# Layer 2 attention: the order of the transfers, of GpSimd's keys and values, and the tiles in which VectorE and ScalarE norm the values

## The chip, the cores and the metric

The kernel runs on one core of a Trainium2 chip, in one launch. The metric is the device time in microseconds (us), taken as the median of the executions shown. The engines are TensorE (PE; its weight loads are shown apart, as PEld), VectorE (DVE), ScalarE (ACT), GpSimd (POOL) and SyncE (SP), which issues the transfers that the 16 DMA engines carry out.

## The reference, cut to what matters

The model is four layers of cross attention and feed-forward on `x` (16 batches, 56 rows, 128 columns), with a context `ctx_1024` of 1500 rows for each batch. The change touches only the attention of layer 2:

```python
xn = _ln(x, ln1_s, ln1_b)
cn = _ln(context, lnc_s, lnc_b)      # every context row: minus its mean, over its deviation
q = xn @ Wq
k, v = jnp.split(cn @ Wkv, 2, axis=-1)
...                                   # 16 heads of 64; one null key and null value in front
sim = jnp.einsum('bhid,bhjd->bhij', q * scale, k)
attn = softmax(where(mask, sim, max_neg))
out = jnp.einsum('bhij,bhjd->bhid', attn, v)
return _ln(out @ Wo, lno_s, lno_b)
```

The kernel folds the weights into the queries and into the output, so that it attends straight to the normed context: the keys are the normed context turned (128 by 1500), the values the normed context as it lies (1500 by 128).

## The kernel before, in words

The 16 heads of 56 queries of a batch are 896 rows, or seven tiles of 128, so the 16 batches make 112 tiles. The 1500 context rows of a batch are 12 chunks of 125 rows. A chunk is cut into four windows: window 0, 1 and 2 have 32 rows, window 3 has the 29 that are left (`LAST_KEYS`) and the null row. A buffer `V` holds the values of one batch: four quadrants of 32 partitions with the same rows in each, and 48 blocks, 12 for each window.

Each of TensorE, VectorE and ScalarE runs one loop over 120 passes. In pass n TensorE makes the scores of tile n (8 matmuls, `scores`, L1628), then one seventh of the weighted sum of the batch that lies eight tiles back (`weigh`, L1647, 56 or 48 small matmuls, the blocks in their order). VectorE takes the maximum of tile n (L1837), turns tile n-1 (L1854), inverts the sum of tile n (L1859), and then norms a window of values if one is due. ScalarE takes the exponentials of tile n (L1764), scales it (L1769), and norms its part of the same window. The scores of a tile wait for the maximum of the tile before it (one PSUM bank). A window of values is normed by three engines: GpSimd takes five chunks of its 12, VectorE three, ScalarE four, in place in `V`. In which pass VectorE and ScalarE do so is set by `values_due`; GpSimd runs a list of its own.

SP issues every transfer in one written order and waits in that order. The waits are these:

- `load_values(b, w)` (L1559) waits until the blocks of window w of the batch before have been weighed, since `V` is one buffer; it is four DMAs, one for each quadrant, of 32 rows, and of 29 rows for window 3.
- `load_keys(b)` (L1573) waits until the scores of batch b-2 are done (two buffers); it is a DMA of 112 rows and one of 15.
- `load_moments(b)` (L1581) brings the means and the reciprocal deviations, spread over all partitions, into single buffers, and waits until GpSimd has normed the keys of batch b-1.
- `load_mask(b)` (L1565) waits until ScalarE has made the mask of batch b-1.

GpSimd norms the keys of a batch with two instructions over 1500 columns (L1713, L1715), and its five chunks of a window with one copy and five instructions (L1720, L1723).

**Words used below.** The cycle of batch v runs from the issue of its window 3 to the issue of window 3 of batch v+1. SP issues it when TensorE has ended the last seventh of batch v-1. Counted from there, TensorE weighs batch v in passes 1 to 7 of the cycle: pass 1 needs window 0, pass 2 window 1, pass 4 window 2 and pass 6 window 3. A pass of TensorE starts a seventh only when all three engines have normed each window that it touches.

The line that says in which pass a window is normed before (n counts all passes, RT is 7):

```python
b, t = divmod(n - RT - 5, RT)
return [(b + 1, t // 2)] if 0 <= b and b + 1 < B and t % 2 == 0 else []
```

In passes of a cycle this is: window 2 of batch v in pass 2, window 3 in pass 4, window 0 of batch v+1 in pass 5, window 1 in pass 7.

Of the kernel before, what the change touches and what calls it, by code (L numbers as in the profile page):

```python
# [14 lines left out]
B, Q, S2 = 16, 56, 1500  # L15
# [101 lines left out]
def ln_pool(pool, k, s):  # L117
    nc = k.nc
    for h in range(2):
        pool.wait_ge(s.ln_var, h + 1)  # L120
        nc.gpsimd.tensor_tensor(k.rstd[:, 4 * h:4 * h + 4], k.mv[:, 4 * h:4 * h + 4, 1], k.half_neg[0:TT, 0:4],
                                ALU.pow).then_inc(s.ln_rstd, 1)
# [768 lines left out]
class LatentAhead:  # L891
# [24 lines left out]
    def load_mask(self, sp, b):  # L916
        sp.dma_start(self.MR[:, b % 2, :], self.src["mask_some"][b].partition_broadcast(TT)).then_inc(self.mask_loaded[b % 2], 16)
# [477 lines left out]
RT = 7  # L1395
WINDOWS = 4
# [76 lines left out]
def attention_16_wide_heads(nc, k, src, ahead):  # L1473
# [8 lines left out]
    with ExitStack() as ctx:  # L1482
# [55 lines left out]
        def values_due(n):  # L1538
            if n < WINDOWS:
                return [(0, n)]  # L1540
            b, t = divmod(n - RT - 5, RT)
            return [(b + 1, t // 2)] if 0 <= b and b + 1 < B and t % 2 == 0 else []

        def step_blocks(g):
            return range(RT * g, min(RT * g + RT, BLOCKS))
# [3 lines left out]
        @block.sync  # L1549
        def _(sp):  # L1550
            def load_values(b, w):
                if b:
                    last_step = (NCH * w + NCH - 1) // RT
                    sp.wait_ge(s.pv_done, RT * (b - 1) + last_step + 1)
                else:
                    sp.wait_ge(s.v_zeroed, 1)
                n = BW if w < WINDOWS - 1 else LAST_KEYS
                for a in range(4):
                    sp.dma_start(V[a * BW:a * BW + n, w * NCH:(w + 1) * NCH, :], src["ctx"][b][w * BW:w * BW + n]  # L1559
                                 ).then_inc(values_loaded[w], 16)  # L1560

            def load_mask(b):
                if b:
                    sp.wait_ge(s.mask_ready, 2 * b)
                sp.dma_start(MR[:], src["mask_full"][b].partition_broadcast(P)).then_inc(s.mask_loaded, 16)  # L1565

            def load_keys(b):
                if b < 2:
                    sp.wait_ge(s.slot_ready, 2 * b + 2)
                else:  # L1570
                    sp.wait_ge(s.scores_filled, RT * (b - 1))
                for rows in (slice(0, TT), slice(TT, P - 1)):
                    sp.dma_start(KT[rows, b % 2, 0:S2], src["ctxT"][b][rows]).then_inc(keys_loaded[b % 2], 16)  # L1573

            def load_moments(b):
                if b == 1:
                    sp.wait_ge(s.q_filled, 2 * H)
                if b:
                    sp.wait_ge(s.keys_scaled, b)
                for x, to in enumerate((MEAN[:], scale_of(b))):  # L1580
                    sp.dma_start(to, scratch[x, b].rearrange("c n -> (c n)").partition_broadcast(P)).then_inc(s.spread_loaded, 16)  # L1581

            load_mask(0)
            load_keys(0)
            sp.wait_ge(s.moments_ready, 1)
            sp.dma_start(scratch.rearrange("k (h b) c n -> (b c) (k h) n", h=2), MOMENTS).then_inc(s.moments_stored, 16)
            sp.wait_ge(ahead.s.means_ready, 1)
            sp.wait_ge(ahead.s.spread, B)
            sp.wait_ge(s.stats_zeroed, 1)
            sp.wait_ge(s.moments_stored, 16)  # L1590
            load_moments(0)
            for x, of in enumerate((ahead.means, rs)):
                for w in range(WINDOWS):
                    n = BW if w < WINDOWS - 1 else LAST_KEYS
                    for a in range(4):
                        sp.dma_start(VST[a * BW:a * BW + n, x, w], of[w * BW:w * BW + n]).then_inc(s.stats_spread, 16)
            load_values(0, 0)
            for a in range(4):
                at = a * BW + LAST_KEYS
                sp.dma_start(V[at:at + 1, BLOCKS - 1, :], k.ident[P - 1:P, :]).then_inc(s.null_rows, 16)  # L1600
            load_values(0, 1)
            load_keys(1)
            load_values(0, 2)
            load_values(0, 3)
            load_moments(1)
            load_mask(1)
            load_mask(2)
            for b in range(1, B):
                if b + 1 < B:
                    load_keys(b + 1)  # L1610
                    load_moments(b + 1)
                for w in range(WINDOWS):
                    if w == WINDOWS - 1 and b + 2 <= B - 1:
                        load_mask(b + 2)
                    load_values(b, w)

        @block.tensor
        def _(pe):
# [86 lines left out]
        @block.gpsimd  # L1705
        def _(pool):
            def normalise_keys(b):
                pool.wait_ge(keys_loaded[b % 2], 32 * (b // 2 + 1))
                pool.wait_ge(s.spread_loaded, 32 * (b + 1))
                if b == 0:  # L1710
                    pool.wait_ge(s.slot_ready, 4)
                keys = KT[0:P - 1, b % 2, 0:S2]
                nc.gpsimd.tensor_tensor(keys, keys, MEAN[0:P - 1], ALU.subtract).then_inc(s.keys_moved, 1)  # L1713
                pool.wait_ge(s.keys_moved, b + 1)
                nc.gpsimd.tensor_tensor(keys, keys, scale_of(b)[0:P - 1], ALU.mult).then_inc(s.keys_scaled, 1)  # L1715

            def normalise_values(b, w):
                pool.wait_ge(values_loaded[w], 64 * (b + 1))
                blocks = slice(w * NCH, (w + 1) * NCH)
                nc.gpsimd.tensor_copy(V[:, blocks, P - 1:P], NULL[:, blocks].unsqueeze(2))  # L1720
                for c in POOL_CHUNKS:
                    x = V[:, w * NCH + c, 0:P - 1]
                    last = nc.gpsimd.tensor_scalar(x, x, VST[:, 1, w, b, c:c + 1], VST[:, 0, w, b, c:c + 1], ALU.mult, ALU.add)  # L1723
                last.then_inc(s.v_pool, 1)

            for u in range(2):
                nc.gpsimd.memset(KT[:, u, :], 0.0).then_inc(s.slot_ready, 1)
                pool.wait_ge(s.slot_ready, 2 * u + 1)
                nc.gpsimd.tensor_copy(KT[:, u, S2:S2 + 1], k.ident[:, P - 1:P]).then_inc(s.slot_ready, 1)
                if u == 0:  # L1730
                    ln_pool(pool, k, s)
                    pool.wait_ge(s.ln_rstd, 2)
            nc.gpsimd.memset(VST[:, :, WINDOWS - 1], 0.0).then_inc(s.stats_zeroed, 1)
            nc.gpsimd.memset(V[:, (WINDOWS - 1) * NCH:, :], 0.0).then_inc(s.v_zeroed, 1)
            nc.gpsimd.memset(BIG[:], FLT_MAX).then_inc(s.constants, 1)
            for u in range(2):
                nc.gpsimd.memset(MA[:, u, WINDOWS - 1, :, LAST_KEYS:BW], FLT_MAX).then_inc(s.margins, 1)
            for u in range(2):
                pool.wait_ge(s.margins, u + 1)
                nc.gpsimd.memset(MA[:, u, WINDOWS - 1, NCH - 1, LAST_KEYS:LAST_KEYS + 1], 0.0).then_inc(s.margins, 1)  # L1740
            pool.wait_ge(s.margins, 4)
            normalise_keys(0)
            pool.wait_ge(s.offsets_ready, 1)
            pool.wait_ge(s.null_column, 2)
            pool.wait_ge(s.null_rows, 64)
            normalise_values(0, 0)
            normalise_values(0, 1)
            normalise_keys(1)
            normalise_values(0, 2)
            normalise_values(0, 3)  # L1750
            for b in range(1, B):
                if b + 1 < B:
                    normalise_keys(b + 1)
                for w in range(WINDOWS):
                    normalise_values(b, w)
            ln_pool(pool, k, s2)

        @block.scalar
        def _(act):
# [51 lines left out]
            for n in range(TILES + LAG):  # L1811
                b, t = divmod(n, RT)
                if n < TILES:
                    exp(n)
                if n >= LAG and (n - LAG) % RT == RT - 1:
                    take_heads((n - LAG) // RT)
                if n < TILES:
                    scale(n)
                if t == (2 if b == 0 else 5) and b + 1 < B:
                    mask(b + 1)  # L1820
                if n == 0:
                    act.wait_ge(s.offsets_ready, 1)
                for v in values_due(n):
                    normalise_values(*v)
# [901 lines left out]
```

## Time and profile before

| | us |
|---|---|
| median of 3 runs | 2388.59 (2386.11 to 2388.67) |
| time of the profiled execution | 2392.87 |
| its span | 2391.1 |
| PE busy / DVE / ACT / POOL | 2023.3 / 1519.9 / 1354.4 / 902.6 |

The span runs from the first to the last instruction; the time has 1.8 us around it. The mean granted TensorE clock is 0.902 of full speed. Layer 2's loop over the tiles lies between 893.7 and about 1816 us of the span.

How rows are read: in the views in order of time a row has its start, its length, engine, line, operation, what it writes and reads, and the count of instructions joined in the row; the brackets hold the idle time of the engine just before it and what ended that. In the view by line, the busy time and the mean time (ns) of one instruction come first, then the idle time before all of them with what ended it. In the view of stretches a row has the bounds, the length, the busy time of PE, PEld, DVE, ACT and POOL with counts of instructions, the granted clock (PEclk, a share of full speed), the mean busy share of the 16 DMA engines and their GB/s. In the list of transfers a row has the count, the size of one and the median us to landing.

### The profile page before, as it was taken

To read this page: it belongs to the slowest core of one execution; us is meant where nothing else is said; L and a number is where in the kernel's file an instruction comes from. 1 tells how busy PE (TensorE), PEld (TensorE's weight loads), DVE (VectorE), ACT (ScalarE), POOL (GpSimd) and SP (SyncE) were. 2 spreads that over 40 slices of the span, in tenths; PEclk is the share of its full clock that TensorE was granted. 3 is DMA by queue.
4 is the path that set the end of the run, shared out by engine and by line. 5 is a ranking of instruction groups with operands and counts; after the bars stand their busy time and mean duration, and the time that the engine had idled before them with its cause. 6 is when DMAs were issued, how large, how long until landed. Compare 5 with 4: busy or idle time off the path is not lost. (4 is left out here: it accounts for less than half of the span.)

```text
span 2391.1 us, 52296 instructions
## 1 busy us (share of the span) xinstructions
PE 2023.3 (85%) x21121; PEld 1414.8 (59%) x21121; DVE 1519.9 (64%) x2958; ACT 1354.4 (57%) x2425; POOL 902.6 (38%) x728
## 2 busy tenths in 40 slices
PE   6999999669998995977777777777785979999996
PEld 3777777458874563645455555555563447777774
DVE  5777778689865435655555565555541667777784
ACT  5787787436662226655556555555540247777763
POOL 7656562057764632122223333222210053434410
PEclk7999999679998987988888888888898879999998
DMA  6454543234412142433333333333320144444430
GB/s 167 139 154 138 145 135 95 76 83 138 125 44 73 36 112 82 114 96 95 96 95 97 94 109 96 94 94 94 92 59 6 36 138 136 141 128 135 128 94 9
DMA packets 105519, 240.03 MB, mean 100 GB/s; under 512 B 45688, under 2 KB 54928, under 8 KB 105024
## 3 DMA queue, kind: packets, MB, share of 16 engines
q1 hardware_dynamic: 105280, 236.69, 34.9%
q8 instruction: 168, 2.75, 0.5%
q14 instruction: 71, 0.58, 0.1%
HBM read 155.38 MB, written 0.65 MB: 65 GB/s over the span
## 5 line engine op out<-in xcount | busy, mean ns | idle before, releaser
L1628 PE MATMUL L2ps<-L2keys,L2qz 128*128 128x384 f32 x896 | 382.3, 576 | 206.1 <-DVE L2negmax L1837 206.0
L1628 PEld LDWEIGHTS L2ps<-L2keys,L2qz 128*128 128x128 f32 x896 | 186.0, 218 | 360.7 <-DVE L2negmax L1837 218.6
L1647 PE MATMUL L2ps<-L2work,L2values 32*128 32x224 f32 x6144 | 325.3, 358 | 21.6 <-POOL L2values L1723 15.8
L1647 PEld LDWEIGHTS L2ps<-L2work,L2values 32*128 32x128 f32 x6144 | 287.9, 188 | 87.9 <-issue 54.8
L1764 ACT ACTIVATE L2work<-L2work,L2negmax 128x1536 f32<-128x1536 f32 x112 | 176.0, 1571 | 164.1 <-DVE L2negmax L1837 164.1
L1854 DVE STREAM_TRANSPOSE L2work<-L2work 128x1568 f32<-128x1568 f32 x112 | 202.6, 1809 | 85.0 <-PE L2ps L1647 83.3
L1837 DVE CUSTOM_DVE_ANT_0 L2work<-L2ps,L2maskadd,L2big 128x1536 f32<-128x1536 f32 x112 | 203.3, 1815 | 77.9 <-PE L2ps L1628 74.3
L1846 DVE TENSOR_SCALAR L2values<-L2values,L2value_stats 128x127 f32<-128x127 f32 x192 | 105.8, 607 | 215.7 <-DMA L2values<-in_ctx 215.7
L1720 POOL COPY L2values<-L2null_column 128x12 f32<-128x12 f32 x64 | 13.1, 204 | 602.1 <-DMA L2values<-in_ctx 585.8
L654 ACT ACTIVATE L3probsT<-L3ps 128x448 f32<-128x448 f32 x384 | 196.1, 547 | 70.9 <-PE L3ps L511 66.4
L654 ACT ACTIVATE L0probsT<-L0ps 128x448 f32<-128x448 f32 x384 | 198.2, 552 | 47.8 <-PE L0ps L511 46.7
L1769 ACT ACTIVATE L2work<-L2work,L2rinv 128x1536 f32<-128x1536 f32 x112 | 176.7, 1577 | 84.1 <-DVE L2rinv L1859 83.9
L1775 ACT ACTIVATE L2values<-L2values,L2value_stats 128x127 f32<-128x127 f32 x256 | 104.4, 481 | 155.1 <-DMA L2values<-in_ctx 155.1
L798 DVE TENSOR_REDUCE L0partmax<-L0ps 112x1 f32<-112x1000 f32 x128 | 153.4, 1198 | 58.8 <-PE L0ps L484 56.7
L798 DVE TENSOR_REDUCE L3partmax<-L3ps 112x1 f32<-112x1000 f32 x128 | 153.4, 1198 | 57.8 <-PE L3ps L484 55.5
L1723 POOL TENSOR_SCALAR L2values<-L2values,L2value_stats 128x127 f32<-128x127 f32 x320 | 147.3, 472 | 0.0
L511 PEld LDWEIGHTS L0ps<-L0query_stack,L0key_stack 99*128 99x128 bf16 x1536 | 110.5, 99 | 56.7 <-issue 12.9
L511 PEld LDWEIGHTS L3ps<-L3query_stack,L3key_stack 98*128 98x128 bf16 x1536 | 110.4, 99 | 54.5 <-issue 13.6
L511 PE MATMUL L0ps<-L0query_stack,L0key_stack 99*128 99x112 bf16 x1536 | 133.7, 214 | 1.3 <-ACT L0probsT L654 1.3
L511 PE MATMUL L3ps<-L3query_stack,L3key_stack 98*128 98x112 bf16 x1536 | 133.2, 214 | 0.0
L605 POOL TENSOR_TENSOR L3keys<-L3keys,L3key_parts 128x1500 f32<-128x1500 f32 x16 | 48.6, 3037 | 193.1 <-ACT L3key_parts L701 193.1
L793 DVE TENSOR_REDUCE L0partmax<-L0ps 112x1 f32<-112x500 f32 x128 | 86.2, 674 | 32.7 <-PE L0ps L476 32.7
(484 smaller groups left out, 4075.1 us busy)
## 6 DMA issues: line engine op xcount, KB each, us to landing
L2values<-in_ctx SPq DMA_DIRECT2D x192, 192.0 KB, 3.8
L0key_stack<-L0key_parts SPq DMA_DIRECT2D x192, 187.5 KB
L3key_stack<-L3key_parts SPq DMA_DIRECT2D x192, 187.5 KB
L0ctxT<-in_ctxT SPq DMA_DIRECT2D x16, 750.0 KB, 4.3
L1rawT<-in_ctxT SPq DMA_DIRECT2D x16, 750.0 KB, 6.5
L2mean_spread<-L_moments SPq DMA_DIRECT2D x16, 750.0 KB, 7.4
L3ctxT<-in_ctxT SPq DMA_DIRECT2D x16, 750.0 KB, 4.5
L2wqk<-L_moments SPq DMA_DIRECT2D x15, 750.0 KB, 27.1
```

The costliest lines, as they stand in the source:

```text
L511: last = nc.tensor.matmul(PS[:, bank, c * TT:(c + 1) * TT], KS[:, h % 4, tau, key_columns(4 * j + c)], QS[:, h % 4, tau, :], start=True, s ...
L654: ins = nc.scalar.activation(PT[:, h % 2, 4 * j:4 * j + 4, tau, :], PS[:, bank, 0:HALF].rearrange("p (c n) -> p c n", c=4), ACT.Exp)
L798: nc.vector.tensor_reduce(PM[:, h % 2, tau, 1:2], PS[0:TT, 1:3, 0:500], AX.XY, ALU.max).then_inc(s.m12_done, 1)
L1628: last = nc.tensor.matmul(PS[:, score_bank(m) + w, 0:NCH * BW], tile_rows(m), key_window(b, w), start=True, stop=True)
L1647: last = nc.tensor.matmul(PS[:, 4 + a, 0:RT * BW], V[a * BW:(a + 1) * BW, n, :], block_cells(a, b, n), start=n == 0, stop=n == BLOCKS - 1, ...
L1723: last = nc.gpsimd.tensor_scalar(x, x, VST[:, 1, w, b, c:c + 1], VST[:, 0, w, b, c:c + 1], ALU.mult, ALU.add)
L1764: nc.scalar.activation(SM[:, m % 2, 0:NPR], SM[:, m % 2, 0:NPR], ACT.Exp, bias=nmax[:, m % 4:m % 4 + 1], scale=-1.0, accum_out=ssum[:, m % ...
L1769: nc.scalar.mul(SM[:, m % 2, 0:NPR], SM[:, m % 2, 0:NPR], rinv[:, m % 4:m % 4 + 1]).then_inc(s.scaled, 1)
L1775: last = nc.scalar.activation(x, x, ACT.Identity, bias=VST[:, 0, w, b, c:c + 1], scale=VST[:, 1, w, b, c:c + 1])
L1837: nc.vector.tensor_tensor_reduce(SM[:, m % 2, 0:NPR].rearrange("p (w n) -> p w n", w=WINDOWS), PS[:, bank:bank + 4, 0:NCH * BW], MA[:, m / ...
L1846: last = nc.vector.tensor_scalar(x, x, VST[:, 1, w, b, c:c + 1], VST[:, 0, w, b, c:c + 1], ALU.mult, ALU.add)
L1854: nc.vector.transpose(turned_cells(b, t), SM[:, m % 2].rearrange("p (g r n) -> p g r n", g=RT, n=BW)).then_inc(s.turned, 1)
```

## The change

No instruction is added or removed. SP's list, GpSimd's list and the passes of `values_due` are put in another order.

```diff
--- before.py
+++ after.py
@@ -1538,8 +1538,8 @@
         def values_due(n):
             if n < WINDOWS:
                 return [(0, n)]
-            b, t = divmod(n - RT - 5, RT)
-            return [(b + 1, t // 2)] if 0 <= b and b + 1 < B and t % 2 == 0 else []
+            b, t = divmod(n - RT - 6, RT)
+            return [(b + 1, (0, 2, 4, 5).index(t))] if 0 <= b and b + 1 < B and t in (0, 2, 4, 5) else []
 
         def step_blocks(g):
             return range(RT * g, min(RT * g + RT, BLOCKS))
@@ -1604,15 +1604,23 @@
             load_values(0, 3)
             load_moments(1)
             load_mask(1)
+            load_moments(2)
             load_mask(2)
-            for b in range(1, B):
+            for b in range(1, B + 1):
+                ahead_of = b + 2 < B
                 if b + 1 < B:
                     load_keys(b + 1)
-                    load_moments(b + 1)
-                for w in range(WINDOWS):
-                    if w == WINDOWS - 1 and b + 2 <= B - 1:
-                        load_mask(b + 2)
-                    load_values(b, w)
+                if b >= 2:
+                    load_values(b - 1, 2)
+                    load_values(b - 1, 3)
+                if b < B:
+                    load_values(b, 0)
+                if ahead_of:
+                    load_moments(b + 2)
+                if b < B:
+                    load_values(b, 1)
+                if ahead_of:
+                    load_mask(b + 2)
 
         @block.tensor
         def _(pe):
@@ -1748,11 +1756,15 @@
             normalise_keys(1)
             normalise_values(0, 2)
             normalise_values(0, 3)
-            for b in range(1, B):
+            for b in range(1, B + 1):
                 if b + 1 < B:
                     normalise_keys(b + 1)
-                for w in range(WINDOWS):
-                    normalise_values(b, w)
+                if b >= 2:
+                    normalise_values(b - 1, 2)
+                    normalise_values(b - 1, 3)
+                if b < B:
+                    normalise_values(b, 0)
+                    normalise_values(b, 1)
             ln_pool(pool, k, s2)
 
         @block.scalar
```

SP, from one batch to the next in the middle of the loop. Before, it issues the keys (two DMAs), the moments (two), windows 0 to 2 of the values (twelve), the mask, and window 3 (the four of 29 rows):

```order
L1573 DMA L2keys<-in_ctxT 112x1500
L1573 DMA L2keys<-in_ctxT 15x1500
L1581 DMA L2mean_spread<-L_moments 128x1500
L1581 DMA L2wqk<-L_moments 128x1500
L1559 DMA L2values<-in_ctx 32x1536 x12
L1565 DMA L2mask<-in_mask_full 128x1500
L1559 DMA L2values<-in_ctx 29x1536 x4
```

After, the keys are followed by window 2 and window 3 of one batch, window 0 of the next, the moments for the batch after that, window 1, and the mask:

```order
L1573 DMA L2keys<-in_ctxT 112x1500
L1573 DMA L2keys<-in_ctxT 15x1500
L1559 DMA L2values<-in_ctx 32x1536 x4
L1559 DMA L2values<-in_ctx 29x1536 x4
L1559 DMA L2values<-in_ctx 32x1536 x4
L1581 DMA L2mean_spread<-L_moments 128x1500
L1581 DMA L2wqk<-L_moments 128x1500
L1559 DMA L2values<-in_ctx 32x1536 x4
L1565 DMA L2mask<-in_mask_full 128x1500
```

So window 3 no longer stands ahead of the keys and the moments but between the keys and window 0; the moments are asked for one batch earlier and stand behind window 0.

ScalarE, from the pass in which it takes the weighed heads out of PSUM (the copies; pass 7 of a cycle), before. The rows with 128x127 are norms, those of 128x1536 the exponentials and the scaling of a tile:

```order
L1781 COPY L2qz<-L2ps 128x7x32 x4
L1769 ACTIVATE L2work<-L2work,L2rinv 128x1536
L1775 ACTIVATE L2values<-L2values,L2value_stats 128x127 x4
L1764 ACTIVATE L2work,L2sums<-L2work,L2negmax 128x1536
L1769 ACTIVATE L2work<-L2work,L2rinv 128x1536
L1764 ACTIVATE L2work,L2sums<-L2work,L2negmax 128x1536
L1769 ACTIVATE L2work<-L2work,L2rinv 128x1536
L1775 ACTIVATE L2values<-L2values,L2value_stats 128x127 x4
L1764 ACTIVATE L2work,L2sums<-L2work,L2negmax 128x1536
L1769 ACTIVATE L2work<-L2work,L2rinv 128x1536
L1764 ACTIVATE L2work,L2sums<-L2work,L2negmax 128x1536
L1769 ACTIVATE L2work<-L2work,L2rinv 128x1536
```

And after:

```order
L1793 COPY L2qz<-L2ps 128x7x32 x4
L1781 ACTIVATE L2work<-L2work,L2rinv 128x1536
L1776 ACTIVATE L2work,L2sums<-L2work,L2negmax 128x1536
L1781 ACTIVATE L2work<-L2work,L2rinv 128x1536
L1787 ACTIVATE L2values<-L2values,L2value_stats 128x127 x4
L1776 ACTIVATE L2work,L2sums<-L2work,L2negmax 128x1536
L1781 ACTIVATE L2work<-L2work,L2rinv 128x1536
L1776 ACTIVATE L2work,L2sums<-L2work,L2negmax 128x1536
L1781 ACTIVATE L2work<-L2work,L2rinv 128x1536
L1787 ACTIVATE L2values<-L2values,L2value_stats 128x127 x4
L1776 ACTIVATE L2work,L2sums<-L2work,L2negmax 128x1536
L1781 ACTIVATE L2work<-L2work,L2rinv 128x1536
```

Window 1 is normed in pass 1 in place of pass 7 of the cycle before, window 2 in pass 3 in place of pass 2. Window 3 stays in pass 4 and window 0 moves from pass 5 to pass 6. VectorE's norms stand in the same passes as ScalarE's.

GpSimd, at the start of the loop, from the keys of batch 2 on. Before, four windows follow the keys:

```order
L1713 TENSOR_TENSOR L2keys<-L2keys,L2mean_spread 127x1500
L1715 TENSOR_TENSOR L2keys<-L2keys,L2wqk 127x1500
L1720 COPY L2values<-L2null_column 128x12
L1723 TENSOR_SCALAR L2values<-L2values,L2value_stats 128x127 x5
L1720 COPY L2values<-L2null_column 128x12
L1723 TENSOR_SCALAR L2values<-L2values,L2value_stats 128x127 x5
L1720 COPY L2values<-L2null_column 128x12
L1723 TENSOR_SCALAR L2values<-L2values,L2value_stats 128x127 x5
L1720 COPY L2values<-L2null_column 128x12
L1723 TENSOR_SCALAR L2values<-L2values,L2value_stats 128x127 x5
```

After, two windows follow (0 and 1 of batch 1), and then the next keys:

```order
L1721 TENSOR_TENSOR L2keys<-L2keys,L2mean_spread 127x1500
L1723 TENSOR_TENSOR L2keys<-L2keys,L2wqk 127x1500
L1728 COPY L2values<-L2null_column 128x12
L1731 TENSOR_SCALAR L2values<-L2values,L2value_stats 128x127 x5
L1728 COPY L2values<-L2null_column 128x12
L1731 TENSOR_SCALAR L2values<-L2values,L2value_stats 128x127 x5
L1721 TENSOR_TENSOR L2keys<-L2keys,L2mean_spread 127x1500
L1723 TENSOR_TENSOR L2keys<-L2keys,L2wqk 127x1500
```

From there on GpSimd norms the keys of batch v+2 ahead of window 2 and 3 of batch v; before, it normed them behind window 3.

## Rows read from the trace of the kernel before

**Rows 1.** Groups by line, tile loop, 893.7 to 1816.2 us.

```profile
L1628 PE MATMUL L2ps<-L2keys,L2qz 128*128 128x384 f32 x896 | 382.3, 576 | 206.1 <-DVE L2negmax L1837 206.0
...
L1846 DVE TENSOR_SCALAR L2values<-L2values,L2value_stats 128x127 f32<-128x127 f32 x192 | 105.8, 607 | 215.7 <-DMA L2values<-in_ctx 215.7
```

**Rows 2.** VectorE in order of time, 1293 to 1314 us.

```profile
1295.21 0.12 DVE L1859 RECIPROCAL L2rinv<-L2sums 128x1 f32<-128x1 f32 x1
...
1306.29 0.86 DVE L1846 TENSOR_SCALAR L2values<-L2values,L2value_stats 128x127 f32<-128x127 f32 x3 [10.96 <-DMA L2values<-in_ctx]
...
1313.64 5.36 DVE L1846 TENSOR_SCALAR L2values<-L2values,L2value_stats 128x127 f32<-128x127 f32 x3 [2.86 <-DMA L2values<-in_ctx]
```

**Rows 3.** SP's transfers in order of time, 1262 to 1328 us.

```profile
1270.61 4.14 SPq L1559 DMA_DIRECT2D L2values<-in_ctx  x4
1274.80 8.70 SPq L1573 DMA_DIRECT2D L2keys<-in_ctxT  x2
...
1286.61 32.55 SPq L1559 DMA_DIRECT2D L2values<-in_ctx  x12
...
1327.90 3.91 SPq L1559 DMA_DIRECT2D L2values<-in_ctx  x4
```

**Rows 4.** Stretches: busy by engine, granted clock, DMA share, GB/s.

```profile
1271.40:1281.80 10.40, 10.40 (x127) 7.38 (x125) 7.41 (x11) 8.24 (x15) 0.00 (x0) 1.00 0.07 26
...
1300.00:1305.80 5.80, 0.00 (x0) 0.00 (x0) 0.00 (x0) 0.00 (x0) 0.00 (x0) 0.88 0.06 26
```

**Rows 5.** TensorE in order of time, 1265 to 1345 us.

```profile
1265.16 2.91 PE L1628 MATMUL L2ps<-L2keys,L2qz 128*128 128x384 f32 x8 [2.38 <-DVE L2negmax L1837]
...
1308.94 5.49 PE L1628 MATMUL L2ps<-L2keys,L2qz 128*128 128x384 f32 x8 [9.90 <-DVE L2negmax L1837]
...
1320.79 4.56 PE L1628 MATMUL L2ps<-L2keys,L2qz 128*128 128x384 f32 x8 [3.40 <-DVE L2negmax L1837]
...
1339.19 2.92 PE L1628 MATMUL L2ps<-L2keys,L2qz 128*128 128x384 f32 x8
1342.04 2.93 PE L1647 MATMUL L2ps<-L2work,L2values 32*128 32x224 f32 x56
```

**Rows 6.** SP issues the last window: batches 1, 14 and 15.

```profile
986.46 3.36 SPq L1559 DMA_DIRECT2D L2values<-in_ctx  x4
...
1730.07 4.62 SPq L1559 DMA_DIRECT2D L2values<-in_ctx  x4
...
1777.22 3.85 SPq L1559 DMA_DIRECT2D L2values<-in_ctx  x4
```

**Rows 7.** VectorE norms those windows: batches 14 and 15.

```profile
1763.88 0.85 DVE L1846 TENSOR_SCALAR L2values<-L2values,L2value_stats 128x127 f32<-128x127 f32 x3 [9.10 <-DMA L2values<-in_ctx]
...
1807.08 0.86 DVE L1846 TENSOR_SCALAR L2values<-L2values,L2value_stats 128x127 f32<-128x127 f32 x3 [25.24 <-DMA L2values<-in_ctx]
```

**Rows 8.** Transfers issued, 986 to 1730 us: count, size, landing.

```profile
L2values<-in_ctx SPq DMA_DIRECT2D x156, 192.0 KB, 3.6
...
L2wqk<-L_moments SPq DMA_DIRECT2D x13, 750.0 KB, 27.1
...
L2keys<-in_ctxT SPq DMA_DIRECT2D x13, 656.2 KB, 11.6
```

**Rows 9.** ScalarE in order of time, 1343 us.

```profile
1342.77 1.63 ACT L1775 ACTIVATE L2values<-L2values,L2value_stats 128x127 f32<-128x127 f32 x4
```

**Rows 10.** Stretches, for the granted clock (columns as in 4).

```profile
1304.40:1314.60 10.20, 5.66 (x12) 2.78 (x16) 5.44 (x8) 7.09 (x11) 5.27 (x7) 0.50 0.06 27
...
1260.00:1304.00 44.00, 36.65 (x432) 26.09 (x432) 26.92 (x33) 24.12 (x33) 10.22 (x20) 1.00 0.46 122
```

**Rows 11.** GpSimd in order of time, 1306 to 1318 us.

```profile
1311.86 3.37 POOL L1713 TENSOR_TENSOR L2keys<-L2keys,L2mean_spread 127x1500 f32<-127x1500 f32 x1 [3.01 <-DMA L2wqk<-L_moments]
1315.31 3.36 POOL L1715 TENSOR_TENSOR L2keys<-L2keys,L2wqk 127x1500 f32<-127x1500 f32 x1
```

## The prediction

> **What bounds the kernel now.** First I read the groups by line over layer 2's loop. TensorE stands idle 206.1 us before its scores, nearly all of it until VectorE's maximum; and VectorE stands idle 215.7 us before its norms of values, all of it until a transfer of values lands [rows 1]. So the loop waits for transfers, through VectorE. Next VectorE in order of time, in one cycle: it is free at 1295.33, waits 10.96 us for window 3, norms it at 1306.29, goes through one tile, and waits another 2.86 us for window 0 of the next batch, whose norm then takes 5.36 us where window 3's took 0.86 [rows 2].
>
> SP's own order says when these were asked for: window 3 at 1270.61, so it takes 35.7 us to land; the keys, the moments and window 0 (1286.61) follow, and the next window 3 comes at 1327.90 [rows 3]. Why so long? In the stretches in which nothing else moves the DMA engines are busy for 0.07 and 0.06 of their time, at 26 GB/s; one of 16 is 0.06. In the last of these stretches no compute engine does anything [rows 4]. So window 3 runs on one DMA engine: 4 x 29 rows x 6144 B = 713 KB at 26 GB/s are 27.4 us, and everything asked for later with a share on that engine lands behind it.
>
> This case is one for a rule of the Trainium skill ("DMA: Bandwidth & Descriptors", section "Why a DMA increments its semaphore by 16 and not by 1"): a transfer is spread over the largest number of engines up to 16 that divides its outer size, which for 29 is 1. It speaks against the change, which leaves the 29 rows as they are. With the page's rate of some 27 GiB/s the window alone would take an estimated 24.6 us in place of 27.4, and my sum below would be about 13 x 2.8 = 36 us lower; the measured rate decides.
>
> TensorE's own work is the other bound. In undisturbed passes it goes without a gap: scores from 1339.19, weighing from 1342.04, 2.85 + 2.86 = 5.71 us a pass [rows 5]. Seven are 40.0 us at most, against a cycle of (1730.07 - 986.46)/13 = 57.2 us [rows 6]. So some 17 us of each cycle are to be had at most.
>
> **The change, in one cycle.** I count from the issue of window 3 (time 0) to its landing (L), and from L to the next issue.
>
> *0 to L.* The wait on which SP issues window 3 is the same as before. What changes is what moves beside it. Before: keys, moments, window 0 and 1, with 35.7 us to landing. Batch 14's window 3 has only window 0 and 1 beside it (no further keys or moments exist), and takes 1763.88 - 1730.07 = 33.8 us [rows 6, 7]. Batch 15's, with nothing after it, takes 1807.08 - 1777.22 = 29.9 us [rows 6, 7]. After the change it is window 0, moments, window 1; the keys go ahead of it. By size, keys are 656 + 88 (15 rows of 6000 B) KB and moments 2 x 750 KB, so the moments are two thirds of what they add together [rows 8]: L = 33.8 + 2/3 x 1.9 = 35.1 us, between 33.8 and 35.7.
>
> *The two norms that move closer.* Window 1 and 2 are now normed in passes 1 and 3 and needed in passes 2 and 4. ScalarE norms last in its pass: in a pass where window 2 was normed it begins at 1342.77 and ends at 1344.40, while TensorE is ready to weigh at 1342.04 [rows 5, 9]. Before, that did not matter (two passes to spare). Now TensorE waits 2.36 us, twice a cycle. Behind the waiting weighing stand the next scores, and VectorE's turn of the tile waits for the weighing too; so VectorE reaches window 3 at 24.7 (1295.33 - 1270.61) + 4.7 = 29.4 us. That is still before L = 35.1. The two waits are hidden by the wait for window 3, which shrinks from 11.0 to 5.7 us. Without that cover they would cost 13 x 4.7 = 61 us.
>
> *L to the next issue.* Before 1327.90 - 1306.29 = 21.6 us [rows 2, 3]. In it lie the wait for window 0 (2.86) and its slow norm (4.5 over 0.86). After, window 0 is normed one pass later, and its 32 rows stand directly behind window 3: a sixteenth of its 4 x 32 rows, eight of 6144 B, is on the slow engine, 1.9 us. The trace has a cycle that shows this case: after batch 14's window 3 VectorE neither waits for window 0 nor norms it slowly, and the next issue comes 1777.22 - 1763.88 = 13.3 us later [rows 6, 7]. There the last pass had no scores to make, which are 2.85 us [rows 5]: 16.2 us. In it the first scores run at half clock (5.49 as in 1308.94, in place of 2.92) since TensorE had idled; the granted clock there is 0.50 [rows 5, 10]. After 2.38 us of idle the scores kept full speed; after 9.90 us they did not, nor after 3.40 us shortly behind another idle stretch [rows 5]. TensorE's idle stretch is now about 4.4 us: its work of passes 1 to 5 ends at 5 x 5.71 + 4.7 = 33.3 us, and it goes on 2.6 us after L (norm and maximum). That is between the rows, so I take the middle of 13.6 (full clock) and 16.2: 14.9 us.
>
> *What is moved and costs nothing.* SP: the keys' two transfers now stand ahead of window 2 and 3. Before, issuing the keys took 8.70 us, behind window 3's 116 rows on one engine [rows 3]. Now at L + 8 us only the tail of window 0, the moments and window 1 (32 rows, 7.5 us) has been there, so I take no delay; the upper bound is that same 8.70 us. The moments wait for GpSimd's keys, done about 4 us into the cycle, ahead of window 0's own wait (pass 2). Window 1 lands about L + 7.5 and is needed 15 us later. GpSimd: 6.7 us of keys [rows 11] now stand ahead of window 2, which is wanted in pass 4, over 20 us on. The mask is made in pass 5 on ScalarE, in another pass than a norm. Each of these has more than 10 us of cover; if the cover fails, what comes late is the weighing of pass 2 or 4.
>
> *Sum.* A cycle is 35.1 + 14.9 = 50.0 us in place of 57.2, 7.2 less, in 13 cycles: 94 us. The start (to 986.46), batch 14's cycle and the end, which already lack what is removed, I leave as they are. From the profiled execution's own 2392.87 that is 2299; it stands 4.3 us over the median, so the forecast is 2295 us. Bounds: 33.8 + 13.6 = 47.4 (gain 127, 2261 us) and 35.7 + 16.2 = 51.9 (gain 69, 2320 us).
>
> **The rivals.**
> - *The norms land under GpSimd's keys.* The slow norm of 5.36 us lay wholly beside the two key instructions [rows 2, 11]. Window 0's norm will come about L + 10 to 13, the keys from about L + 12; window 1's norm at 7.6 us of the cycle, the keys end near 4. If both collide, that is 2 x 4.5 = 9.0 us, of which the rest of the wait for window 3 (5.7) hides part: 3.3 x 13 = 43 us lost, 2338 us. One collision alone is hidden. The Trainium skill has a rule for it ("SBUF — State Buffer", "Who interferes with whom"): VectorE's tensor_scalar and GpSimd take turns at one pair of ports, and the later one is shut out for the whole instruction; the 5.36 us agree.
> - *Window 3 lands much sooner*, as batch 15's did: L = 29.9. Then it meets VectorE at 29.4, nearly no idle time is left, the clock stays up: 29.9 + 13.6 = 43.5 us, 13.7 x 13 = 178 us, 2210 us. Against it: 3.1 MB still move beside it.
> - *SP reaches window 3 late.* It now stands behind the mask, the keys and window 2, all asked for within 8 us of the landing. If the keys' issue is held up as before (8.7) and window 2's too (4.6 as window 3's own [rows 6]), window 3 is asked for at L + 8 + 13.3 = L + 21.3 in place of 14.9: 6.4 us late, 11 us gained in all, no change worth naming. From 7.2 us on it is slower; at 10 us 13 x 2.8 = 36 us, 2425 us. Against it: the engine that held the issues up is nearly empty then.
>
> **Chances.** The forecast (2261 to 2320) 0.62; the collisions (to 2345) 0.13; the early landing (2210 to 2261) 0.13; the late issue 0.12, of which 0.03 still faster, 0.04 no change, 0.05 slower. By 0.2%, or 4.8 us (about what these runs can tell from no change): faster 0.91, same 0.04, slower 0.05. The range from 2240 to 2345 leaves out about half of the early landings and the late issues.
>
> **What would show it.** Right: the wait before VectorE's norm of window 3 falls to 4 to 7 us in each cycle; the wait for window 0 and its 5 us norm are gone; TensorE has two new waits of about 2.4 us a cycle before weighing, put down to ScalarE or the values; window 3 takes 34 to 36 us to land. Wrong: window 3's landing leaves that span, or its issue comes more than 0.5 us after the end of the last weighing, or norms of 4 to 5 us remain.

## The result and the profile after

The changed kernel takes 2306.41 us (median of 4 runs, 2304.93 to 2308.43). The kernel before, measured beside it, takes 2387.82 (4 runs, 2386.11 to 2388.67). The ratio is 0.9661, with a 95% interval of 0.9644 to 0.9677: 81 us faster. The forecast was 2295 us, 94 us faster. The profiled execution took 2306.95, 85.9 less than that of before. Its page begins so (busy time, share of the span, instructions):

```profile
span 2305.2 us, 52296 instructions
...
PE 2006.2 (87%) x21121; PEld 1412.6 (61%) x21121; DVE 1470.6 (64%) x2958; ACT 1351.8 (59%) x2425; POOL 903.1 (39%) x728
```

The new lines in the code are L1636 for the scores, L1655 for the weighing, L1787 for ScalarE's norm and L1858 for VectorE's. The mean granted clock is 0.930, before 0.902. In order of time, VectorE's norms of window 3 and of the next window 0 in one cycle (SP asked for this window 3 at 1240.49):

```profile
1276.00 0.85 DVE L1858 TENSOR_SCALAR L2values<-L2values,L2value_stats 128x127 f32<-128x127 f32 x3 [4.40 <-DMA L2values<-in_ctx]
...
1286.33 0.84 DVE L1858 TENSOR_SCALAR L2values<-L2values,L2value_stats 128x127 f32<-128x127 f32 x3
```

Against [rows 2], the wait of 10.96 has become 4.40, the wait of 2.86 is gone, and window 0's norm takes 0.84 us in place of 5.36. Window 3 itself still takes 1276.00 - 1240.49 = 35.5 us, before 35.7. The waits over the 13 cycles, by engine and line (total, times, longest):

```profile
POOL L2keys L1721 <- DMA L2keys<-in_ctxT: 81.7, 13, 11.8
PE L2ps L1655 <- ACT L2values L1787: 59.9, 25, 2.4
DVE L2values L1858 <- DMA L2values<-in_ctx: 57.7, 13, 6.4
```

VectorE waits for transfers of values 13 times, 4.4 us on average; before, the same view gave 181.4 us in 26 waits. The second line is new: TensorE waits 2.40 us, 25 times, for ScalarE's norm, and once more, at 1198.36, where the profile puts the same wait down to GpSimd: two in each of the 13 cycles. TensorE in order of time:

```profile
1265.24 4.39 PE L1655 MATMUL L2ps<-L2work,L2values 32*128 32x224 f32 x56 [2.40 <-ACT L2values L1787]
1269.56 3.09 PE L1636 MATMUL L2ps<-L2keys,L2qz 128*128 128x384 f32 x8
1272.58 2.93 PE L1655 MATMUL L2ps<-L2work,L2values 32*128 32x224 f32 x56
1278.64 2.91 PE L1636 MATMUL L2ps<-L2keys,L2qz 128*128 128x384 f32 x8 [3.13 <-DVE L2negmax L1849]
...
1316.23 2.93 PE L1655 MATMUL L2ps<-L2work,L2values 32*128 32x224 f32 x56 [2.39 <-ACT L2values L1787]
...
1329.66 5.39 PE L1636 MATMUL L2ps<-L2keys,L2qz 128*128 128x384 f32 x8 [4.79 <-DVE L2negmax L1849]
```

The weighing at 1265.24, behind a wait of 2.40, takes 4.39 us; the one at 1316.23, behind 2.39, takes 2.93. The scores behind window 3 run in 2.91 after an idle time of 3.13 and in 5.39 after 4.79. The view of stretches shows the clock under the slow weighing, and under the loop as a whole (columns as in [rows 4]):

```profile
1266.60:1270.00 3.40, 3.40 (x37) 2.86 (x30) 0.26 (x1) 0.10 (x2) 0.00 (x0) 0.51 0.07 27
1270.00:1278.00 8.00, 5.50 (x64) 3.75 (x63) 3.60 (x6) 3.22 (x5) 1.97 (x5) 1.00 0.45 113
984.40:1645.21 660.81, 554.62 (x5721) 386.03 (x5722) 378.28 (x520) 404.02 (x560) 207.53 (x338) 0.94 0.40 108
```

0.51 is the lower of the two levels (1.2 of 2.4 GHz). From the first row too: while window 3 is alone on its way, the DMA engines are still busy for 0.07 at 27 GB/s, as in [rows 4]. The last row is 13 cycles, 660.81 / 13 = 50.8 us each. SP in order of time around the issues:

```profile
1283.77 0.35 SPq L1565 DMA_DIRECT2D L2mask<-in_mask_full  x1
1284.15 0.91 SPq L1573 DMA_DIRECT2D L2keys<-in_ctxT  x2
1285.11 11.12 SPq L1559 DMA_DIRECT2D L2values<-in_ctx  x8
```

The keys are issued in 0.91 us, where they took 8.70 behind window 3's rows [rows 3].

### The profile page after: what moved, and what is told of

The parts are those of the page before. It is cut to its first block and busy times, and to the rows that moved or that the text cites. A ratio compares the mean times of both kernels' runs of the same rounds, so it can differ in the third digit from the quotient of the medians.

```text
span 2305.2 us, 52296 instructions
## 1 busy us (share of the span) xinstructions
PE 2006.2 (87%) x21121; PEld 1412.6 (61%) x21121; DVE 1470.6 (64%) x2958; ACT 1351.8 (59%) x2425; POOL 903.1 (39%) x728
## 5 line engine op out<-in xcount | busy, mean ns | idle before, releaser
L1655 PE MATMUL L2ps<-L2work,L2values 32*128 32x224 f32 x6144 | 346.8, 375 | 86.9 <-ACT L2values L1787 64.7
L1636 PE MATMUL L2ps<-L2keys,L2qz 128*128 128x384 f32 x896 | 347.9, 532 | 64.8 <-DVE L2negmax L1849 64.8
L1655 PEld LDWEIGHTS L2ps<-L2work,L2values 32*128 32x128 f32 x6144 | 308.0, 198 | 151.0 <-issue 119.6
L1636 PEld LDWEIGHTS L2ps<-L2keys,L2qz 128*128 128x128 f32 x896 | 170.1, 200 | 205.5 <-DVE L2negmax L1849 72.5
L1787 ACT ACTIVATE L2values<-L2values,L2value_stats 128x127 f32<-128x127 f32 x256 | 104.4, 479 | 61.0 <-DMA L2values<-in_ctx 61.0
L1858 DVE TENSOR_SCALAR L2values<-L2values,L2value_stats 128x127 f32<-128x127 f32 x192 | 58.7, 362 | 82.7 <-DMA L2values<-in_ctx 82.7
```

Of the source, the lines that this page charges most:

```text
L1636: last = nc.tensor.matmul(PS[:, score_bank(m) + w, 0:NCH * BW], tile_rows(m), key_window(b, w), start=True, stop=True)
L1655: last = nc.tensor.matmul(PS[:, 4 + a, 0:RT * BW], V[a * BW:(a + 1) * BW, n, :], block_cells(a, b, n), start=n == 0, stop=n == BLOCKS - 1, ...
L1787: last = nc.scalar.activation(x, x, ACT.Identity, bias=VST[:, 0, w, b, c:c + 1], scale=VST[:, 1, w, b, c:c + 1])
```

## The experiments

Two theories stood against each other. Theory 1 is the prediction's: window 3, on one DMA engine, bounds the cycle; what moves beside it and behind it sets the rest; the two norms that come closer to their use are hidden. Theory 2: one part alone brings the gain. Each run is beside the kernel before; "loop" is layer 2's cycles 1 to 13.

**The change with the passes of before** (e1), to see what `values_due` adds:

```diff
-            b, t = divmod(n - RT - 6, RT)
-            return [(b + 1, (0, 2, 4, 5).index(t))] if 0 <= b and b + 1 < B and t in (0, 2, 4, 5) else []
+            b, t = divmod(n - RT - 5, RT)
+            return [(b + 1, t // 2)] if 0 <= b and b + 1 < B and t % 2 == 0 else []
```

> The changed kernel with one part undone: VectorE and ScalarE norm the values in the passes of before (window 2 in pass 2, window 3 in pass 4, window 0 in pass 5, window 1 in pass 7); SP's and GpSimd's new orders stay. Theory 1 (a cycle is the landing of window 3, about 35.4 us on one DMA engine, plus the way from there to its next issue; TensorE's two new waits are hidden in the first part): TensorE's waits before weighing vanish, the wait for window 3 grows back to about 10.5 us, the first scores after it run at half clock every time: 35.4 + 16.2 = 51.6 us a cycle, 10 us more in all: 2305 to 2320 us. Theory 2 (the passes are what pays, the orders of SP and GpSimd add little): over 2350 us.

Measured: 2307.83 us, before 2385.01, ratio 0.9672 [0.9652, 0.9692]. Within the interval this is the whole gain. VectorE in order of time:

```profile
1248.64 4.29 DVE L1858 TENSOR_SCALAR L2values<-L2values,L2value_stats 128x127 f32<-128x127 f32 x3
...
1281.99 0.85 DVE L1858 TENSOR_SCALAR L2values<-L2values,L2value_stats 128x127 f32<-128x127 f32 x3 [6.46 <-DMA L2values<-in_ctx]
```

Window 1's norm (1248.64) now lies beside GpSimd's keys (1245.77 to 1252.61) and takes 4.29 us; TensorE's waits of 2.4 us are gone. Either is hidden under the wait for window 3. That wait was expected at 10.5 us; it is 6.46 here and 6.9 on average, since the expectation left the slow norm out. So in this kernel the new passes trade one hidden delay for another.

**The passes alone** (e2): before, with only `values_due` changed (the diff above, turned round).

> The kernel before with the new passes of VectorE's and ScalarE's norms alone. Theory 1: window 0, which lands about 7.4 us after window 3, is normed a pass later (10 to 13 us after it), so its wait and most of its slow norm go, while the two waits of TensorE are hidden: about 35.7 + 15.5 = 51 us a cycle, so this part alone has nearly the whole gain: 2305 to 2330 us. Theory 3 (the order of the transfers is what pays; the parts add up): over 2350 us.

Measured: 2350.81 us, ratio 0.986 [0.9839, 0.9881], 20 us above the expected range. The wait for window 0 is gone and its norm is down to about 1.2 us, as expected. But from window 3's landing to the next issue it takes 17 to 20 us (17.8 on average), not 15.5, and window 3 lands after 36.4 us on average, not 35.7. GpSimd and then TensorE in order of time:

```profile
1297.79 3.37 POOL L1713 TENSOR_TENSOR L2keys<-L2keys,L2mean_spread 127x1500 f32<-127x1500 f32 x1 [3.01 <-DMA L2wqk<-L_moments]
1301.24 3.36 POOL L1715 TENSOR_TENSOR L2keys<-L2keys,L2wqk 127x1500 f32<-127x1500 f32 x1
```

```profile
1304.75 4.54 PE L1628 MATMUL L2ps<-L2keys,L2qz 128*128 128x384 f32 x8 [2.54 <-POOL L2keys L1715]
```

Pass 7 of the cycle begins the scores of a new batch, so the new keys are needed there. They wait for the moments, which land behind window 3. TensorE waits 2.54 us for GpSimd and then runs its scores at 4.54 us.

**SP's order alone** (e3): the change with both `values_due` and GpSimd's list as before. GpSimd's part:

```diff
-            for b in range(1, B + 1):
+            for b in range(1, B):
                 if b + 1 < B:
                     normalise_keys(b + 1)
-                if b >= 2:
-                    normalise_values(b - 1, 2)
-                    normalise_values(b - 1, 3)
-                if b < B:
-                    normalise_values(b, 0)
-                    normalise_values(b, 1)
+                for w in range(WINDOWS):
+                    normalise_values(b, w)
```

> The kernel before with SP's new order alone; GpSimd's list and the passes of the norms as before. Theory 1: window 0 stands directly behind window 3 and lands 2 us after it, so the wait for it goes; but GpSimd's keys now come right behind its own norm of window 3, just where VectorE norms window 0 in pass 5, so the slow norm of about 5 us stays. Window 3 lands somewhat sooner (33 to 35 us), since the moments wait for GpSimd. About 33.5 + 18.4 = 52 us a cycle: 2310 to 2340 us. If the parts add up: the gain of this run and of the passes alone would sum to about 81 us; by theory 1 to about 130 us or more.

Measured: 2352.44 us, ratio 0.9864 [0.9845, 0.9883]; 12 us above the expected range. SP in order of time up to the issue of a window 3, VectorE after it, and a stretch:

```profile
1301.77 0.34 SPq L1581 DMA_DIRECT2D L2mean_spread<-L_moments  x1
1302.16 0.43 SPq L1581 DMA_DIRECT2D L2wqk<-L_moments  x1
1302.63 2.09 SPq L1559 DMA_DIRECT2D L2values<-in_ctx  x4
1304.77 0.52 SPq L1565 DMA_DIRECT2D L2mask<-in_mask_full  x1
1305.33 0.93 SPq L1573 DMA_DIRECT2D L2keys<-in_ctxT  x2
1306.30 1.85 SPq L1559 DMA_DIRECT2D L2values<-in_ctx  x4
```

```profile
1347.43 0.86 DVE L1854 TENSOR_SCALAR L2values<-L2values,L2value_stats 128x127 f32<-128x127 f32 x3 [13.32 <-DMA L2values<-in_ctx]
...
1351.84 4.21 DVE L1854 TENSOR_SCALAR L2values<-L2values,L2value_stats 128x127 f32<-128x127 f32 x3
```

```profile
1300.00:1310.00 10.00, 8.52 (x111) 6.18 (x104) 8.12 (x9) 6.12 (x9) 4.21 (x7) 1.00 0.75 225
```

In SP's new list the moments stand ahead of window 1, the mask, the keys and windows 2 and 3, and they wait for GpSimd's keys. With GpSimd's old list those keys come behind window 3, so SP is held, and then issues everything in a bunch (0.75 of the DMA engines, 225 GB/s) directly ahead of window 3, at 1309.33. That one takes 1347.43 - 1309.33 = 38.1 us in place of 35.7 before. That the bunch is what lengthens it is inferred from the order of these rows. The slow norm of window 0 (4.21 us) is there as expected. Over the 13 cycles the landing takes 37.7 us on average, expected 33.5, and the way from there to the next issue 16.6, expected 18.4.

**GpSimd's list alone** (e7): before, with the diff of the last experiment turned round.

> The kernel before with GpSimd's new list alone (keys of batch v+2 ahead of window 2 and 3 of batch v), SP's order and the passes as before. Theory 1 (GpSimd's list pays only because SP asks for keys and moments a batch earlier): SP still asks for the keys behind window 3, so GpSimd stands waiting for them with window 2 and 3 queued behind; window 2 is normed about 14.5 us after window 3 has landed, TensorE's pass 4 waits for it, a cycle is near 35.7 + 34 = 70 us: 2500 to 2600 us, slower than before. Rival (keys first on GpSimd is a gain by itself): below 2388 us.

Measured: 2563.74 us, before 2387.23, ratio 1.0726 [1.0698, 1.0753], a cycle of 70.3 us: as expected. Its waits:

```profile
POOL L2keys L1713 <- DMA L2wqk<-L_moments: 582.9, 12, 49.2
...
PE L2ps L1647 <- POOL L2values L1723: 313.5, 11, 29.1
```

GpSimd now waits for the moments with window 2 and 3 behind it in its list, while SP's old list asks for those moments only after window 3. TensorE then waits up to 29.1 us for GpSimd's values.

So the parts do not add: passes alone 34 us gained, SP alone 33, GpSimd alone 176 lost, SP and GpSimd together 77, all three 81.

**Window 3 cut for more DMA engines** (e4). This tests the bound itself: the kernel before, with each transfer of 29 rows as one of 16 and one of 13, and nothing else changed but the counts that are waited for.

```diff
-                n = BW if w < WINDOWS - 1 else LAST_KEYS
-                for a in range(4):
...
+                for r, n in ((0, BW),) if w < WINDOWS - 1 else ((0, 16), (16, LAST_KEYS - 16)):
+                    for a in range(4):
...
-                pool.wait_ge(values_loaded[w], 64 * (b + 1))
+                pool.wait_ge(values_loaded[w], (128 if w == WINDOWS - 1 else 64) * (b + 1))
```

> The kernel before, with each of window 3's four transfers of 29 rows cut into one of 16 rows and one of 13 rows; all orders as before. Theory 1 (29 rows run on one DMA engine, and this bounds the cycle): window 3 lands within about 8 us, VectorE no longer waits for any transfer in the loop, a cycle falls to TensorE's 39.6 us plus at most 3.5 where a norm meets GpSimd's keys: 2135 to 2185 us. If the landing time is not due to the 29 rows but to the traffic beside it: 2370 us or more.

Measured: **2124.76 us** (2123.14 to 2127.57), before 2385.01, ratio 0.8909 [0.8892, 0.8926], 10 us better than the expected range. A stretch of the loop, the norm of the last batch's window 3 by VectorE, and a stretch in which that window is on its way without the other windows:

```profile
1060.00:1440.00 380.00, 380.00 (x4221) 265.51 (x4219) 282.74 (x387) 294.82 (x408) 157.15 (x254) 1.00 0.60 143
```

```profile
1532.98 0.85 DVE L1846 TENSOR_SCALAR L2values<-L2values,L2value_stats 128x127 f32<-128x127 f32 x3 [3.79 <-DMA L2values<-in_ctx]
```

```profile
1528.30:1530.30 2.00, 2.00 (x28) 1.89 (x24) 0.89 (x3) 1.44 (x4) 2.00 (x5) 0.50 0.97 134
```

TensorE is busy for all of the 380 us at full clock; a cycle is 39.55 us, TensorE's own work. VectorE's wait for the last window, 25.24 us in [rows 7], is 3.79. The cut also makes eight transfers of four, but the last row shows what differs: the DMA engines are busy for 0.97 of their time at 134 GB/s, where the uncut window alone has 0.06 to 0.07 and 26 [rows 4]; that is five times the rate, not sixteen. In the stretch of the loop the old order of transfers, lists and passes costs nothing once the window lands in time. This version beats both kernels, the changed one by 182 us.

**The same cut in the changed kernel** (e5), and **in it with the passes of before** (e6). Here the cover of the new passes is taken away.

> The changed kernel with window 3's four transfers of 29 rows cut into 16 and 13 rows. Theory 1 (in the changed kernel TensorE's two waits of 2.4 us a cycle cost nothing only because the landing of window 3 hides them): the landing no longer binds, so the waits stand open: 39.6 + 4.7 us a cycle, and up to 3 us more where TensorE's clock falls behind them, in 14 cycles: 2185 to 2240 us, 60 us or more above the kernel before with the same cut (2125). Rival (the new passes and orders help by themselves): not above 2125 us.

> The same cut of window 3, with SP's and GpSimd's new orders and VectorE's and ScalarE's norms in the passes of before. Theory 1: no wait for a transfer and none before weighing; what may remain is that window 1's norm in pass 7 meets GpSimd's keys (3.4 to 5.6 us in the run with the passes put back), of which TensorE's lead hides some: 39.6 to 43 us a cycle, 2115 to 2175 us, so at or above the kernel before with the cut and under the changed kernel with it. Rival (the new orders help by themselves): below 2115 us.

Measured: e5 2200.12 us, before 2387.23, ratio 0.9227 [0.9172, 0.9282]; e6 2169.04 us, ratio 0.9064 [0.9028, 0.9099]; both as expected. A stretch of e5, and its waits there:

```profile
1060.00:1440.00 380.00, 339.28 (x3767) 237.01 (x3766) 251.58 (x343) 263.42 (x369) 138.44 (x222) 1.00 0.52 128
```

```profile
PE L2ps L1655 <- ACT L2values L1787: 35.9, 15, 2.4
```

Its cycle is 44.5 us in most batches, 39.55 plus two waits of 2.4: what the prediction said that they cost without a cover. (Two more of these waits in the stretch are put down to GpSimd.) In e6, VectorE, GpSimd (the second of its two key instructions; the first starts at 1188.68) and TensorE in order of time:

```profile
1188.50 7.05 DVE L1858 TENSOR_SCALAR L2values<-L2values,L2value_stats 128x127 f32<-128x127 f32 x3
```

```profile
1192.13 3.34 POOL L1723 TENSOR_TENSOR L2keys<-L2keys,L2wqk 127x1500 f32<-127x1500 f32 x1
```

```profile
1197.34 5.49 PE L1636 MATMUL L2ps<-L2keys,L2qz 128*128 128x384 f32 x8 [5.06 <-DVE L2negmax L1849]
```

Window 1's norm falls on GpSimd's keys, takes 7.05 us, and TensorE waits 5.06 us for the maximum behind it. With the old passes this happens in about every other cycle, most cycles being 39.6 or 46 us. So with a fast window 3 the new lists of SP and GpSimd lose 44 us against e4, and the new passes another 31 (by medians; the four runs of e5 spread from 2195 to 2224).

## Why the prediction was right, step by step

**The bound** held. In the changed kernel window 3 still goes at 27 GB/s while it is alone, and cutting its rows (e4) took away the whole wait. The rule that the prediction weighed (the Trainium skill, "DMA: Bandwidth & Descriptors", section "Why a DMA increments its semaphore by 16 and not by 1") agrees with both: by it 29 rows go to one engine, and 16 and 13 rows to 16 and 13; that it is 16 and 13 no view here shows, only that nearly all engines are busy (0.97).

**The sum.** A cycle was forecast at 50.0 us and is 50.8, before 57.2. The landing of window 3, up to VectorE's norm of it, was forecast at 35.1 and takes 35.6 on average, before 35.8. From there to the next issue 14.9 was forecast; it takes 15.25, before 21.4. So the gain lies behind the landing, as forecast. The loop gives 13 x (57.20 - 50.83) = 83 us; the forecast was 94, and the 0.8 us a cycle are the difference. The loop's start and batch 14's cycle, left as they were in the sum, gave 2.1 and 2.7 us (984.40 in place of 986.46, 44.5 in place of 47.15); the end lost 1.6; and the profiled execution, 4.3 us over the median before, is 0.5 over it after.

Both terms are right on average only, and some of that is luck. The prediction's own signs, a wait of 4 to 7 us before window 3's norm in each cycle and a landing within 34 to 36 us, fail in four and in six of the 13 (waits of 0.15 to 6.4, landings of 31.5 to 37.4). For the landing, the forecast took the keys to be out of the way once they are issued ahead. SP's rows tell the cycles apart. In five of them window 3 is asked for 5.4 to 5.7 us behind the keys and lands after 36.5 to 37.4 us, 37.1 on average; in seven it is asked for 6.8 to 8.5 us behind them and lands after 34.3 to 35.7, on average the 35.1 that were forecast. The keys at 1284.15, shown with the result, are of the first kind (window 3 at 1289.80); these, a cycle later, are of the second (window 3 at 1343.29):

```profile
1335.17 0.91 SPq L1573 DMA_DIRECT2D L2keys<-in_ctxT  x2
```

The thirteenth, batch 13's, has no moments beside its window 3, which the sum did not see; it lands after 31.5 us, and without it the average is 35.9, no sooner than before.

For the way to the next issue, the middle between the two clock levels is what a cycle seldom takes: it is 13.8 us in four cycles (TensorE idle 1.9 to 3.3 us before the scores, which then run in 2.91) and 16.3 to 16.7 in five (idle 4.1 to 4.8, scores 5.4 to 5.5); four lie between (14.7 to 15.4), two of them after idle times of 2.1 and 5.0. The prediction gave no ground for the middle other than that its 4.4 us of idle lay between its rows.

**The two norms that moved closer** made the waits that were forecast (2.40 us, forecast 2.36), and they were hidden; e5 shows the price without cover, 75 us above e4 together with the lists. **Mis-sized** was what follows on them: the prediction took from a 2.38 us idle that the clock survives [rows 5]. In 12 of the 26 cases the weighing behind the wait takes 4.3 to 4.6 us, 4.5 on average, in place of 2.93, one of the two in each cycle but batch 12's. In that cycle VectorE is free for window 3 at 29.7 us, where 29.4 was forecast; in the others at about 31.2. With the landing 0.5 us later than forecast, that leaves a wait for window 3 of 4.4 us in place of 5.7, and the slow weighing is hidden under it too.

**Window 0** went as forecast: no wait, 0.84 us of norm. But the prediction names the later pass and the order of the transfers together, and either is enough: with the passes of before (e1) there is no wait and the norm takes 0.91 us, and with the new passes alone (e2) there is no wait and it takes about 1.2. SP's order without GpSimd's list (e3) removes the wait and leaves the slow norm. The collision, one rival, does not occur for window 0 and 1 in the changed kernel (their norms take 0.8 to 1.8 us), but does for window 1 in e1 and e6 and for window 0 in e3. e1 differs in the passes alone, so they are what keeps window 1's norm away from the keys. That one collision alone is hidden, as the prediction said, e1 shows: it costs nothing that its runs can tell. (The 5.36 us of [rows 2] lay not quite wholly beside the keys: they end 0.3 us later.) The rule on ports named there (the Trainium skill, "SBUF — State Buffer", section "Who interferes with whom") agrees with the norm of 7.05 us, which in e6 lies beside one pair of key instructions.

**The late issue**, the rival on the other side, did not come: the weighing of a batch ends at 1289.7 (1287.19 + 2.55) and window 3 of the next is asked for at 1289.8, and all cycles are alike in this. **The early landing** did not come either while 3.1 MB move beside window 3. Where less does, it lands sooner: batch 13's and 14's windows 3, with windows 0 and 1 alone beside them, are normed after 31.5 and 32.5 us, batch 15's, with nothing, after 29.6.

**What it overlooked:** that the new batch's keys are needed already in pass 7. In the changed kernel they have been ready for long, so the sum was not touched; in e2 their lateness takes back part of the gain. It is most of why my expectation of e2 was too fast, by 20 us: 13 x (17.8 - 15.5) = 30 us behind the landing, against 13 x 0.7 = 9 before it. That of e3, too fast by 12, overlooked that SP is held by the moments.

**Open:** whether the keys' nearness is what makes window 3 land late. The two go together in the 12 cycles above and in e3 (keys 3.3 to 5.0 us ahead, landing 37.3 us or more, batches 2 to 13). Each cycle with 13.8 us behind its landing brings the next window 3 nearer to the keys and is followed by a late landing; so the landing alternates between about 35 and 37 us from batch 4 to 11. No run changes this distance by itself.

## What to carry to other kernels

Before reordering a queue, see at what rate its late transfer moves when it is alone: here one of 16 DMA engines was at work, and a cut of 29 rows into 16 and 13 was worth 260 us, three times what the reordering of three queues gave. Lists of engines that wait for each other are to be moved together: each part alone gave less than half, or lost 176 us, while SP's and GpSimd's together gave nearly all. A delay that is hidden under a wait comes back when that wait is mended: the changed order is 75 us slower than the old one once the window lands in time.

## What the runs showed that I had not expected

Waits of TensorE of the same length (2.39 to 2.40 us) lower the clock in some places and not in others: in 12 of 26 cases in the changed kernel, in none of the first 21 in e5 and then in four in a row. In e5's stretch TensorE idles for nothing else (40.7 us, 17 such waits). Before the scores an idle time of 3.30 us left the clock up (scores in 2.91) and one of 2.08 did not (4.45). So the length of the idle time alone does not decide it; what does was not settled. And issuing transfers on SP takes longer behind a transfer that sits on one DMA engine: the keys' two cost 8.70 us there [rows 3], 0.91 in the changed order, and in e4, directly behind the cut window 3, 1.18:

```profile
1211.12 3.73 SPq L1559 DMA_DIRECT2D L2values<-in_ctx  x8
1214.90 1.18 SPq L1573 DMA_DIRECT2D L2keys<-in_ctxT  x2
```
